# First stage of a two-layer graph and attention kernel: root, turnings, one-hots and chunk splits put in another order

## The reference

```python
xn = _layernorm(x, axis=-1)
x = x + _L0_gnn_ref(xn, node_type_3, edge_index, edge_type_3, ...) + _L0_mix_ref(xn[None], W_qkv, b_qkv, ...)[0]
...
# _L0_mix_ref: 12 heads of 64, 256 random features
qkv = (x @ W_qkv + b_qkv).reshape(b, n, 3, H, D)
phi_q = jax.nn.relu(jnp.einsum('bhnd,md->bhnm', q, random_features))
phi_k = jax.nn.relu(jnp.einsum('bhnd,md->bhnm', k, random_features))
kv = jnp.einsum('bhnm,bhnd->bhmd', phi_k, v)
# _L0_gnn_ref: per relation, the mean over the edges into each node
count = jax.ops.segment_sum(onehot, dst, num_segments=num_nodes)
msg = xw[edge_type, src] * inv[dst, edge_type][:, None]
agg = jax.ops.segment_sum(msg, dst, num_segments=num_nodes)
```

## Time and profile before

| | |
|---|---|
| median of 3 runs | 1956.39 us (1956.12 to 1959.42) |
| the profiled execution | 1959.61 us, span 1957.8 us |
| PE busy | 1875.9 us, 96% |
| DVE busy | 1199.5 us, 61% |
| ACT busy | 875.6 us, 45% |
| mean granted clock of TensorE | 0.989 |

### The profile page before, as it was taken

How to read it: one execution, slowest core, us unless ns; L and a number is a source line. 1 busy time by engine, 2 the same in 40 slices (tenths; PEclk the granted TensorE clock), 3 DMA queues, 4 the chain that set the end, 5 groups by cost and what they waited for, 6 DMA issues and landing times. The chain is left out here.

```text
span 1957.8 us, 31663 instructions
## 1 busy us (share of the span) xinstructions
PE 1875.9 (96%) x12715; PEld 1766.6 (90%) x12715; DVE 1199.5 (61%) x1898; ACT 875.6 (45%) x1189; POOL 97.3 (5%) x97
## 2 busy tenths in 40 slices
PE   5899899999999999998999999899999999999999
PEld 4799799999999999998999999798878888888899
DVE  6667785444333345446457777665666668889732
ACT  5756521222121211224477751423655557777620
POOL 0000000000000000000000101000111101100000
PEclk9999999999999999999999999899999999999999
DMA  4211244221211121120211041424877779999831
GB/s 124 66 49 33 71 122 102 72 57 38 72 43 57 52 81 49 50 62 20 74 33 33 17 154 41 161 84 179 288 239 233 223 230 336 365 380 378 290 119 40
DMA packets 157961, 250.50 MB, mean 128 GB/s; under 512 B 11949, under 2 KB 86189, under 8 KB 157460
## 3 DMA queue, kind: packets, MB, share of 16 engines
q1 hardware_dynamic: 152532, 231.21, 35.4%
q0 software_dynamic: 5040, 17.56, 3.7%
q10 hardware_dynamic: 272, 0.07, 0.0%
HBM read 228.80 MB, written 20.01 MB: 127 GB/s over the span
## 5 line engine op out<-in xcount | busy, mean ns | idle before, releaser
L183 PE MATMUL psum<-products_room 128*128 128x512 f32 (+2 forms) x2160 | 457.2, 366 | 3.2 <-DVE re_credit L3905 2.0
L183 PEld LDWEIGHTS psum<-products_room 128*128 128x128 f32 (+1 forms) x2160 | 388.4, 187 | 47.3 <-issue 2.4
L183 PE MATMUL psum<-ring_hi,xt_sb 128*128 128x256 f32 (+3 forms) x1920 | 358.6, 284 | 10.4 <-DVE a_sb L765 2.8
L3802 DVE TENSOR_TENSOR products_room<-moe_raw,products_room 128x1536 fp32r<-128x1536 f32 x179 | 312.4, 1754 | 79.2 <-ACT products_room L3701 78.9
L3701 ACT ACTIVATE products_room<-moe_raw 128x1536 fp32r<-128x1536 f32 x179 | 266.0, 1489 | 152.6 <-PE psum L183 86.0
L183 PEld LDWEIGHTS psum<-ring_hi,xt_sb 128*128 128x128 f32 (+1 forms) x1920 | 301.8, 189 | 12.5 <-issue 5.9
L183 PE MATMUL psum<-ring_lo,xt_sb 128*128 128x256 f32 (+3 forms) x960 | 271.3, 283 | 0.0
L183 PEld LDWEIGHTS psum<-ring_lo,xt_sb 128*128 128x128 f32 (+1 forms) x960 | 181.5, 189 | 0.0
L183 PE MATMUL psum<-ring_hi,gnn_sb 128*128 128x256 f32 (+1 forms) x810 | 147.5, 283 | 4.5 <-DVE gnn_sb L1213 3.6
L139 DVE TENSOR_TENSOR ring_lo<-ring_raw,ring_hi 128x1536 fp32r<-128x1536 f32 (+1 forms) x64 | 119.4, 1866 | 46.4 <-ACT ring_hi L128 46.3
L191 PE MATMUL psum<-xt_sb,ring_hi 128*128 128x314 f32 x744 | 141.2, 311 | 1.0 <-DVE a_sb L1450 0.7
(11 more groups left out here) (542 smaller groups left out, 2745.2 us busy)
## 6 DMA issues: line engine op xcount, KB each, us to landing
moe_raw<-in_L_ffn_Wg_r SPq DMA_DIRECT2D x60, 768.0 KB, 5.5
moe_raw<-in_L_ffn_Wu_r SPq DMA_DIRECT2D x60, 768.0 KB, 6.8
moe_raw<-in_L_ffn_Wd_r SPq DMA_DIRECT2D x60, 768.0 KB, 8.7
ring_raw<-in_L_gnn_w_rel SPq DMA_DIRECT2D x18, 896.0 KB, 5.0
ring_raw<-in_L_mix_W_qkv SPq DMA_DIRECT2D x24, 384.0 KB, 4.3
ring_raw<-in_L_gnn_w_rel SPq DMA_DIRECT2D x9, 768.0 KB, 4.5
ring_raw<-in_L_gnn_w_root SPq DMA_DIRECT2D x6, 896.0 KB, 4.9
count_total_dram<-gnn_sb POOLq DMA_DIRECT2D x3, 1570.0 KB, 11.6
```

The source lines that it names most:

```text
L183: mm = pe.matmul(out, lhs[a], rhs[b], start=(first and i == 0), stop=(last and i == 2))
L3802: dve.tensor_tensor(wlo[:, i % RING, :], raw[i % RAWS], whi[:, i % RING, :].bitcast(F32), ALU.subtract)\
```

## The change

In `phase_start` ScalarE makes the root before it splits chunk 0. Turnings take three banks in turn (2, 3 and 5) instead of two, so that `turn(i)` waits for `low(i - 3)`, and the queues of ScalarE and VectorE are rearranged so that turnings are read out one value tile ahead. ScalarE makes 22 of the 80 key one-hots instead of 26: every third below 24, every fourth above. It makes three numbers' share of them per value tile (ACT_LEAD) instead of four. VectorE makes its four numbers' share of one-hots ahead of the value sum, and the low half of chunk 1 comes behind value tile 3's low half. In `phase_attend`, for the first layer, the splits of chunks 3 and 4 move behind the first value tiles of their group: ScalarE's behind the second, VectorE's behind the third tile's sum and the second's low half.

```diff
--- before.py
+++ after.py
@@ -624,9 +624,10 @@
                 act.sem_inc(s["v_hi"], TT)
                 qk_high(0, KEYS)
                 qk_high(0, QUERIES)
-                ring_high(act, st, 3)
                 for i in range(TT, 2 * TT):
                     v_high(i)
+                    if i == TT + 1:
+                        ring_high(act, st, 3)
             act.wait_ge(s["rf_bd"], 1)
             act.activation(rf2[:, 0, :], rff, ACT.Copy).then_inc(s["rf_hi"], 1)
             if second:
@@ -638,9 +639,9 @@
                 v_high(2 * TT + 1)
                 ring_high(act, st, 4)
             else:
-                ring_high(act, st, 4)
                 v_high(2 * TT)
                 v_high(2 * TT + 1)
+                ring_high(act, st, 4)
             for i in range(2 * TT + 2, 3 * TT):
                 v_high(i)
             for p in range(PAIRS):
@@ -755,7 +756,7 @@
                 dve.wait_ge(s["v_hi"], i + 1)
                 dve.tensor_tensor(dst, src.rearrange("p (h d) -> p h d", d=DH), hi, ALU.subtract).then_inc(s["v_lo"], 1)
 
-            def values(c):
+            def values(c, n=None):
                 for i in range(c * TT, (c + 1) * TT):
                     t = i - c * TT
                     if not second:
@@ -766,6 +767,8 @@
                                           bv[0:TS[t], c * 256:(c + 1) * 256], ALU.add).then_inc(s["v_f"], 1)
                         if t >= 1:
                             v_low(i - 1)
+                        if t == 2:
+                            ring_low(dve, st, n)
                     else:
                         v_low(i)
                 if not second:
@@ -802,8 +805,7 @@
                 dve.sem_inc(s["v_lo"], TT)
                 qk_low(0, KEYS)
                 qk_low(0, QUERIES)
-                ring_low(dve, st, 3)
-                values(1)
+                values(1, 3)
             dve.wait_ge(s["rf_turned"], 1)
             for hd in range(2):
                 ins = dve.tensor_copy(rff[own(hd), :], k.banks[7][0:DH, 0:MF])
@@ -820,8 +822,7 @@
                 for i in range(2 * TT + 2, 3 * TT):
                     v_low(i)
             else:
-                ring_low(dve, st, 4)
-                values(2)
+                values(2, 4)
             for p in range(PAIRS):
                 if second:
                     dve.wait_ge(s["kn_mm"], p + 1)
@@ -1271,8 +1272,10 @@
 GROUP = 8
 GROUPS = ET // GROUP
 ROW_SLOTS = 4
-ON_ACT = [n for n in range(ET) if n % 3 == 2]
+TURN_BANKS = (2, 3, 5)
+ON_ACT = [n for n in range(24) if n % 3 == 2] + [n for n in range(24, ET) if n % 4 == 3]
 ACT_FIRST = 9
+ACT_LEAD = 3
 TILE_EDGES = 4
 UNIT_EDGES = 5
 BLOCK_DST = 102
@@ -1356,7 +1359,7 @@
 
         def x_turned(i):
             t, j0, j1 = X_TURNS[i]
-            return k.banks[2 + i % 2][:, 0:(j1 - j0) * P].rearrange("p (j n) -> p j n", n=P)[:, :, 0:TS[t]]
+            return k.banks[TURN_BANKS[i % 3]][:, 0:(j1 - j0) * P].rearrange("p (j n) -> p j n", n=P)[:, :, 0:TS[t]]
 
         def value_bank(t):
             return k.banks[7 if t % 2 == 0 else 4][0:TS[t], 0:256]
@@ -1497,24 +1500,27 @@
             normal(0)
             normal(1)
             ring_low(dve, st, 0)
+            low(0)
+            low(1)
+            normal(2)
+            low(2)
+            low(3)
             dve.wait_ge(s["bias_in"], 16)
             for t in range(TT):
-                low(2 * t)
-                low(2 * t + 1)
+                for n in range(TILE_EDGES * t, TILE_EDGES * (t + 1)):
+                    hot(n)
+                if t + 3 < TT:
+                    normal(t + 3)
+                value_sum(t)
                 if t + 2 < TT:
-                    normal(t + 2)
+                    low(2 * t + 4)
+                value_low(t)
+                if t + 2 < TT:
+                    low(2 * t + 5)
                 if t == 3:
                     ring_low(dve, st, 1)
-                for n in range(TILE_EDGES * t, TILE_EDGES * (t + 1)):
-                    hot(n)
-                if t >= 1:
-                    value_sum(t - 1)
-                    value_low(t - 1)
             for n in range(TILE_EDGES * TT, ET):
                 hot(n)
-                if n == TILE_EDGES * TT + 2:
-                    value_sum(TT - 1)
-                    value_low(TT - 1)
                 if n == ET // 2:
                     ring_low(dve, st, 2)
                 for b in dve_blocks:
@@ -1553,22 +1559,23 @@
             act.wait_ge(s["weighed"], 1)
             for n in range(ACT_FIRST):
                 hot(n)
-            ring_high(act, st, 0)
             act.wait_ge(s["var_ready"], 1)
             act.activation(k.root[:], k.ve[:], ACT.Sqrt).then_inc(s["root_ready"], 1)
+            ring_high(act, st, 0)
+            for i in range(4):
+                high(i)
             for t in range(TT):
-                high(2 * t)
-                high(2 * t + 1)
+                first = ACT_FIRST + ACT_LEAD * t
+                for n in range(first, first + ACT_LEAD):
+                    hot(n)
+                value_high(t)
+                if t + 2 < TT:
+                    high(2 * t + 4)
+                    high(2 * t + 5)
                 if t == 2:
                     ring_high(act, st, 1)
-                if t >= 1:
-                    value_high(t - 1)
-                for n in range(ACT_FIRST + TILE_EDGES * t, ACT_FIRST + TILE_EDGES * (t + 1)):
-                    hot(n)
-            for n in range(ACT_FIRST + TILE_EDGES * TT, ET):
+            for n in range(ACT_FIRST + ACT_LEAD * TT, ET):
                 hot(n)
-                if n == ACT_FIRST + TILE_EDGES * TT + 2:
-                    value_high(TT - 1)
                 if n == ET // 2:
                     ring_high(act, st, 2)
                 for b in act_blocks:
@@ -1607,8 +1614,8 @@
             def turn(i):
                 t, j0, j1 = X_TURNS[i]
                 pe.wait_ge(s["xn_ready"], t + 1)
-                if i >= 2:
-                    pe.wait_ge(s["lo_done"], i - 1)
+                if i >= 3:
+                    pe.wait_ge(s["lo_done"], i - 2)
                 for j in range(j0, j1):
                     mm = pe.transpose(x_turned(i)[:, j - j0, :], xn[0:TS[t], t, j * P:(j + 1) * P],
                                       k.ident[0:TS[t], 0:TS[t]])
```

## The result

The changed kernel takes 1946.44 us (median of 7 runs, 1944.36 to 1949.06); the kernel before, run beside it, 1958.24 (7 runs, 1953.64 to 1959.56). The ratio is 0.9942, 95% interval 0.9933 to 0.9951: 11.4 us faster (9.6 to 13.1). The profiled execution took 1946.44 us, span 1944.6.

A forecast was written before the change was run, and what follows sets the result against it. TensorE was taken to bound the kernel, with idle time or a lower clock in two early stretches. First stage 8.2 plus next phase 3.1 made 11.3 us, from the median of 1956.39 to 1945.1 us; range 1941.5 to 1950.

The forecast's parts named there:

- The walk of the first stage: First stage's queues walked from VectorE resuming at 14.70: dense part at 40.4, edge tile 24 at 42.75, 8.2 us gained.
- The pauses: TensorE's new waits ahead of the dense part: 0.7, some 0.9 and 1.4 us, the last ahead of edge tile 16.
- the turnings' waits and the low clock: First stage: TensorE's waits for low halves and 1.2 GHz behind the last, most of the 8.2 us besides the root's 2.7.
- this edit by itself gives nothing but the room for the order above: Dense part: 22 instead of 26 one-hots on ScalarE; both engines keep ahead, so the part takes what it took.
- The next phase: Chunk splits behind two value tiles: TensorE's two waits for VectorE's value sum go, 1.3 and 1.8 us, 3.1 together.
- the 0.9 us for a phase at full clock: Next phase: 0.9 us more if TensorE is at full clock in its first two value tiles; not in the sum.
- A: Ahead of the root: the table load waits for the variance; 1.3 us less gain, 1946.4; chance 0.12 together with a longer switch.
- The longer switch, 2.66 us: Table switch keeps ScalarE from 12.61 until 15.27; kernel at 1945.9; chance 0.12 together with the load waiting for the variance.
- B: The new pauses and the 1.75 us between the phases drop TensorE's clock; some 2.8 us cost, 1948; chance 0.13.
- C: Behind the two stretches, a VectorE chain or transfer gives gains back; a third lost means 1949 to 1950; chance 0.07.
- D: TensorE at full clock in value tile 0 or the next phase's first two; 0.9 to 1.7 us more, 1943.5; chance 0.12.
- E: Clock stays at 1.2 GHz through the dense part; kernel 13.7 us slower, 1970; chance 0.02.

The follow-up runs named there:

- hots_early: Changed kernel with VectorE's key one-hots moved between value sum and low half, chunk 1's low half one value tile earlier; 1943.77 us, ratio 0.9926 to the kernel before.
- root_only: Kernel before with only ScalarE's root ahead of its split of chunk 0; ratio 0.9992.
- order_only: Kernel before with only the first stage's queues in the changed order (two banks, 26 one-hots on ScalarE, root behind the split); ratio 0.9983.
- two_waits: Changed kernel with a second, long since satisfied wait (edges_turned) ahead of ScalarE's root; one run, 1947.05 us.
- attend_only: Kernel before with only phase_attend taken from the changed kernel (chunk splits behind two value tiles); ratio 0.9980.
- banks_only: Kernel before with only a third bank for the turnings; one run, 1959.56 us.
- tuned: Changed kernel with early VectorE one-hots, ScalarE's chunk 1 split one value tile earlier, one-hot 13 on ScalarE, 21 and 22 ahead of value low 4; 1942.49 us, ratio 0.9931.

## Why the prediction was right

The forecast was 1945.1 us, 11.3 us faster; measured were 1946.44 and a ratio that means 11.4.

**The walk of the first stage.** The root was walked to 14.45 and came at 14.65: it waited for one more small instruction of VectorE (L244). VectorE resumed at 14.90 (14.70 forecast), value tile 0 began at 19.95 (19.85), tile 2 at 27.31 (27.65), tile 4 at 35.16 (35.55), the dense part at 40.24 (40.4), edge tile 24 at 42.70 (42.75), 8.2 us as summed. The pauses were forecast at 0.7, 0.9 and 1.4 us. The first is 0.67 ahead of the group and 0.45 between its matmuls (30.96 to 31.81 is 0.85 for a group that takes 0.40 in hots_early, where it doesn't wait), so 1.1. The second is 0.24 and 0.23 in the same way (0.73 for a group that takes 0.50 there), so 0.5. The third is 1.73. That it would be ended by the row one-hots was wrong: the trace names a key one-hot (L1434). By the walk's own costs key one-hot 16 comes 0.31 us behind the row one-hots of 39.02, at 39.33, and edge tile 16 needs both; it ran at 39.28. Value tile 0 took 3.15 us where 3.48 was put, its matmuls having reached the faster pace sooner. So the walk was up to 0.4 us off on the way (tile 4), and a last pause 0.3 longer brought it back: that it meets edge tile 24 within 0.05 us is luck, that it stays within 0.4 all the way is not.

**What is whose.** The prediction laid 2.7 us to the root and most of the rest to the turnings' waits and the low clock. Alone the root gives 2.4 (root_only) and the order 5.0 (order_only), 4.7 without the earlier root of that execution; the third bank gives 0.2 in the old order and 1.1 to 1.25 in the new one. Root, order and bank come to 8.2 to 8.35 us at edge tile 24, where 8.2 were measured together. How the order's 4.7 us divide between the waits and the low clock behind them, no run tells.

**The term left unpriced** is "this edit by itself gives nothing but the room for the order above", on the fewer one-hots. The room was counted at nothing and is worth 2.06 us in the new order; what the edit gives in the old order wasn't run. The figures for a price were there: with 26 entries ScalarE would have had 18 one-hots, a split, three blocks and a value high from 40.3 on, 28.6 us by the prediction's own costs, in 27.4, so 1.2 us too many. The sum came out right all the same, since it was made for the kernel with the edit in. What was wrong is how the gain divides among the parts, not the total.

**The next phase.** 3.1 us were forecast, 3.3 measured (22.96 instead of 26.24 us from first matmul to features; 22.95 in the kernel with this part alone). The changed kernel's clock fell again behind the pause of 1.74 us between the phases (0.93 over the stretch), so the 0.9 us for a phase at full clock were rightly left out.

**The rivals.** A, the table load behind the wait, was excluded by the row at 12.62; two_waits shows its price in this kernel, 1.35 us at the root and 1.44 at the features (forecast 1.3). The longer switch, 2.66 us, would have put the root at 15.27 at the earliest; it came at 14.65. B, the new pauses dropping the clock, came only between the phases, where it had fallen before too: the granted clock is 1.00 from 12.5 to 68 us in spite of waits of 0.67, 0.24 and 1.73 us. C, the gain given back later, didn't come; the rest was 1.7 us shorter. D came in small part, 0.33 us in value tile 0. E didn't.

**The 1.7 us behind the features.** The same 12,200 matmuls are in both. TensorE is busy for 1797.2 us of 1852.2 after, and for 1800.6 of 1853.85 before; the idle time is 55.0 and 53.3. So nothing was waited for less (1.7 us more, in fact); the matmuls themselves took 3.4 us less. That is the clock: by the granted clock of stretches of 10 us, added up, about 28.2 us of that part are at 1.2 GHz after and 34.2 before, and half of the 6.0 us between them is 3.0. Of other kernels here, two_waits has 1796.5 us busy in that part and attend_only 1801.7 (first fence two_waits, second attend_only):

```profile
93.86:1945.30 1851.44, 1796.52 (x12200) 1695.35 (x12198) 1130.16 (x1730) 815.03 (x1097) 93.12 (x78) 0.99 0.40 130
```

```profile
100.67:1956.00 1855.33, 1801.74 (x12200) 1700.34 (x12198) 1131.16 (x1730) 815.23 (x1097) 93.21 (x78) 0.99 0.40 130
```

In the same way 23.9 us are at 1.2 GHz in two_waits and 38.0 in attend_only, so the less of it, the shorter the matmuls took, in all four. TensorE's instructions from there to the end are the same in all of them. Whether a kernel's share of low clock in this part follows from where its first stage ends, or changes from one execution to the next, wasn't settled; one profiled execution of each can't tell.

## What to carry to other kernels

Where a stretch is set by one engine's chain (here VectorE's: statistics, low halves, one-hots), walking its queue instruction by instruction with measured start-to-start costs foretells times to some tenths of a microsecond, and also what each other engine may cost before it matters. A second buffer is worth what the chain behind it can't absorb, 0.2 or over 1 us for the same bank. An edit that looks like bookkeeping (which engine makes which one-hots) must be priced by its undoing: what would the engine have to do in the time that it has, if the edit weren't there? And a difference of some tenths between two single traces is no effect of the edit until the pieces that vary by themselves (here value tile 0, and when the first weights land) have been compared too.

## What the runs showed of the hardware

**A table load passes a single wait, but not the one written last of two.** It ran at 12.62 with one wait written ahead of its activation, and at 14.71 with two. It stood behind the wait written last, here and at 1205.03.

**When the first weights land varies.** ScalarE's split of chunk 0 waited for its transfer until 14.35 in the kernel before, and until 13.28, 13.85 and 14.03 in three kernels whose start is the same. With the root behind the split, the first turning moves with it: 19.15, 18.08, 18.66 and 18.83. What follows need not: in attend_only, whose first stage is that of the kernel before, the turning was 0.49 us earlier and the dense part at 47.88 instead of 47.84. Value tile 0 took 3.99 us there instead of 3.48, and VectorE waited for it:

```profile
27.00 0.42 DVE L1451 TENSOR_TENSOR a_sb<-psum,v_bias 128x256 f32<-128x256 f32 x1 [0.61 <-PE psum L183]
```

With the root ahead of it, behind a single wait, it was 16.66 in each of seven profiled executions (seven kernels). So the root's part is 1.4 to 2.5 us at the first turning, by the execution.

**The clock after the same pause.** The pause between the two phases was 1.74 to 1.78 us in all twelve kernels. Behind it the clock fell to 1.2 GHz in nine of them, the kernel before and the changed one among them, and not in order_only, banks_only and tuned. In order_only TensorE then waited 2.54 us at 81.75 instead of 1.16 for VectorE's value sum, and from the phase's start to the features it took 26.20 us, against 26.24 in the kernel before: where VectorE sets the pace, TensorE's clock can change only how long it waits. In banks_only it didn't end so: behind nearly the same wait, 2.55 us, the clock fell, and the same stretch took 27.79 us (76.47 to 104.26). So neither pause foretells the clock by its length here.
